# Four stages of a twelve-stage decoder kernel: pieces issued by due times, and 23 instead of 24 expert tiles

## The reference, cut to what matters

```python
x = x + _L0_attn_ref(_layernorm(x), ...)      # "memory attention", stage 0
x = x + _L0_xattn_ref(...)
x = x + _L0_ffn_ref(_layernorm(x), ...)       # 4 of 32 experts, stage 2
...
x = x + _L2_ffn_ref(_layernorm(x), ...)       # 1 of 8 experts, stage 8
...
x = x + _L3_ffn_ref(_layernorm(x), ...)       # low-rank layer, stage 11

# stage 2, routing:  scores = sigmoid(tokens @ router.T); best 2 of 4 groups by the sum of
#   their top 2; top 4 experts inside them; weights normalised, times 2.5.
#   Each expert: down(silu(gate x) * up x). A shared expert is added for every token.
# stage 8, routing:  top1 = argmax(x @ gate_W + gate_b)
#   each expert: gelu(x W1[e] + b1[e]) W2[e] + b2[e], only for its own tokens
# stage 11:
logits = einsum('bsd,ed->bse', x, gate_w) + gate_b
top_v, top_i = top_k(softmax(logits), 2);  val_sum = top_v.sum(-1)
for e in range(8):
    gate = (top_i == e).sum(-1) * val_sum
    h = relu(x @ wi.T + bi + (x @ lora_A[e].T) @ lora_B[e].T)      # rank 16, 1024 wide
    out += gate[..., None] * (h @ wo.T + bo)
```

## Time and profile before

| | |
|---|---|
| median of 3 runs | 4128.17 us (4126.56 to 4131.38) |
| profiled execution, own time | 4137.42 us |
| its span, first to last instruction | 4135.9 us |
| granted PE clock, mean | 0.873 |
| PE, DVE, ACT, POOL busy | 3217.4, 2401.6, 1643.8, 1412.9 us |

### The profile page before, as it was taken

The page is one execution under the profiler, slowest core; times in us unless marked ns, Lnnn a source line. Parts: engine busy times, 40 slices in busy tenths (PEclk is TensorE's granted clock), DMA queues, the critical chain, the costliest instruction groups (busy, mean ns, idle before and its releaser), DMA issues. The chain is left out here.

```text
span 4135.9 us, 53041 instructions
## 1 busy us (share of the span) xinstructions
PE 3217.4 (78%) x17661; PEld 2052.2 (50%) x17661; DVE 2401.6 (58%) x6477; ACT 1643.8 (40%) x3713; POOL 1412.9 (34%) x1086
## 2 busy tenths in 40 slices
PE   5888888676890678777699999478779677768898
PEld 3666666554660223322466666345656423325655
DVE  6787887247333799999343443534542258875543
ACT  3566665111120455454244444415602144436511
POOL 3666666210436254555222222301010135540110
PEclk7888888788995799999899999788969878889999
DMA  2000000300444000000000000011121200000000
GB/s 95 5 7 9 6 9 6 138 11 13 118 114 134 17 0 0 0 0 0 16 8 1 1 1 1 11 50 64 40 81 32 59 22 1 0 29 2 2 1 21
DMA packets 71175, 116.36 MB, mean 28 GB/s; under 512 B 28704, under 2 KB 58552, under 8 KB 68160
## 3 DMA queue, kind: packets, MB, share of 16 engines
q1 hardware_dynamic: 61312, 86.76, 6.2%
q0 software_dynamic: 9600, 26.23, 2.6%
HBM read 88.84 MB, written 24.12 MB: 27 GB/s over the span
## 5 line engine op out<-in xcount | busy, mean ns | idle before, releaser
L1210 POOL TENSOR_TENSOR L_attn_state<-L_attn_state,L_attn_ccol 128x1024 f32<-128x1024 f32 x192 | 458.4, 2389 | 456.1 <-DVE L_attn_state L1203 353.4
L1168 PE MATMUL bank<-L_attn_state,ident 128*128 128x512 f32 x768 | 416.2, 668 | 107.3 <-POOL L_attn_state L1210 72.4
L1203 DVE TENSOR_TENSOR_SCAN L_attn_state<-L_attn_decay,bank 128x1024 f32<-128x1024 f32 x192 | 438.6, 2284 | 22.7 <-ACT L_attn_decay L1179 3.5
L1179 ACT ACTIVATE L_attn_decay<-L_attn_dt,L_attn_A 128x512 f32<-128x512 f32 x384 | 256.2, 716 | 206.3 <-DVE L_attn_state L1203 163.3
L1168 PEld LDWEIGHTS bank<-L_attn_state,ident 128*128 128x128 f32 x768 | 152.1, 210 | 279.6 <-issue 123.6
L1107 POOL TENSOR_TENSOR L_xattn_prob<-L_xattn_prob,L_xattn_inv 128x1024 f32<-128x1024 f32 x64 | 121.1, 1893 | 411.9 <-DVE L_xattn_inv L1090 411.9
L1195 DVE TENSOR_TENSOR bank<-L_attn_dtx,bank 128x1024 f32<-128x1024 f32 x192 | 235.6, 1227 | 28.9 <-PE bank L1162 23.7
L1162 PE MATMUL bank<-L_attn_parts,L_attn_select 96*128 96x512 bf16 x384 | 145.4, 418 | 126.7 <-DVE bank L1195 110.1
L1185 ACT COPY L_attn_ccol<-bank 128x512 f32<-128x512 f32 x192 | 110.8, 577 | 208.4 <-PE bank L1162 191.5
L2813 POOL TENSOR_TENSOR L_attn_t<-L_attn_t,L_attn_base 128x1024 f32<-128x1024 f32 x96 | 183.2, 1909 | 21.6 <-DVE L_attn_base L2762 21.6
L1162 PEld LDWEIGHTS bank<-L_attn_parts,L_attn_select 96*128 96x128 bf16 x384 | 38.2, 104 | 291.1 <-DVE bank L1195 178.2
(11 more groups left out here) (599 smaller groups left out, 7551.0 us busy)
## 6 DMA issues: line engine op xcount, KB each, us to landing
L_ffn_ew<-in_L_ffn_experts SPq DMA_DIRECT2D x4, 3072.0 KB, 21.2
L_ffn_made<-L_ffn_yout SPq DMA_DIRECT2D x24, 512.0 KB, 3.0
L_ffn_w<-in_L_ffn_w SPq DMA_DIRECT2D x4, 2048.0 KB, 14.6
L_xattn_ctx<-in_ctx_rows SPq DMA_DIRECT2D x3, 2048.0 KB, 8.7
L_ffn_rows<-L_ffn_xh SPq DMA_DIRECT2D x8, 512.0 KB, 2.9
L_ffn_made<-L_ffn_yout SPq DMA_DIRECT2D x12, 256.0 KB, 2.1
L_attn_rows<-in_x SPq DMA_DIRECT2D x16, 128.0 KB, 6.8
turned<-L_attn_rows SPq DMA_DIRECT2D x16, 128.0 KB, 2.3
```

Source lines behind the costliest of these rows:

```text
L1168: t = pe.matmul(self.y[unit % len(self.y)][m][:, :], self.c.ident[:, :], self.state[N % 3][:, m, :], start=n == 0, stop=n == 15)
L1179: t = act.activation(self.decay[N % 2][:, m, :], dt[:, m, :], ACT.Exp, scale=A[:, m, n:n + 1])
L1203: dve.tensor_tensor_scan(flat(self.state[N % 3]), flat(self.decay[N % 2]), flat(self.drive), 0.0, ALU.mult, ALU.add).then_inc(*self.scanne ...
L1210: pool.tensor_tensor(state[:, :, :], state[:, :, :], self.ccol[N % 2][:, :].unsqueeze(1).broadcast_to([P, 2, GT]), ALU.mult).then_inc(*sel ...
```

## The change

The four stages get their order from tables of due times. A step name that several engines shared is split, so that each engine's part has a due time of its own (`gate`/`logits`, `turn`/`turned`, `up`/`relu`, `out`/`outed`, `top`/`raise`, `base`/`shift`, `exp`/`pick`, `rcopy`/`keep`, `choose`/`hold`, and others). In lora h1 gets a second buffer, and ACT's first relu of a group waits for `out` of two groups before. top1 works on 23 tiles, and the last tile, now without a partner, is written alone. The operations themselves are the same.

```diff
+LORA_BY_GROUP = {"root": -11.65, "stats": -11.01, "norm": -10.84, "turned": (-8.79, -7.89), "turn": (-7.92, -7.03), "logits": -7.82, "choose": -7.11,
+                 "weigh": -7.06, "shift": -6.92, "gate": -6.45, "masked": -5.12, "down": -4.01, "flipped": (-3.3, -1.98), "flip": (-2.23, -1.48),
+                 "up": (-0.86, 1.09, 2.5, 3.04, 3.91, 4.05, 7.46, 8.3), "relu": (-0.68, 1.15, 1.2, 2.49, 4.13, 7.01, 7.89, 8.47),
+                 "add": (-0.12, 0.46, 1.08, 3.47, 4.05, 5.58, 6.15, 8.66), "out": (9.27, 12.19), "outed": (11.22, 12.32)}
...
-    h1, h2 = s.sb("h1", [P, FC, GT]), [s.sb(f"h2{n}", [P, GT]) for n in range(3)]
+    h1, h2 = [s.sb(f"h1{n}", [P, FC, GT]) for n in range(2)], [s.sb(f"h2{n}", [P, GT]) for n in range(3)]
...
-        yield "stats", 0
-        yield from front(0)
-        for g in range(NGROUP):
...
+        yield "begin", 0
+        yield from as_due(due_by(LORA_BY_GROUP, 10, range(NGROUP)))
...
-            if g and m == 0:
-                act.wait_ge(*out.filled(2 * g - 1))
+            if g >= 2 and m == 0:
+                act.wait_ge(*out.filled(2 * (g - 2) + 1))
...
+BY_UNIT = {"score": -0.87, "scopy": 0.32, "top": 0.35, "raise": 0.75, "shift": 0.93, "total": 1.06, "spare": 1.15, "base": 1.24, "log": 1.4,
+           "pick": 1.73, "exp": 1.96, "turn": 2.1, "recall": 2.48, "tcopy": 2.66, "keep": 3.3, "rcopy": 3.55}
+BY_BLOCK = {"xturn": -6.43, "norm": -5.99, "xcopy": -5.4, "qsum": -3.59, "square": -3.4, "scale": -3.17, "qmul": -3.06, "out": 12.98, "y": 13.45,
+            "ynorm": 14.61, "store": 14.84}
+BY_HALF = {"query": (-5.65, -3.93), "qadd": (-4.64, -3.76), "qturn": (-2.92, -2.69), "qcopy": (-2.53, -0.82), "pair": (8.53, 9.32),
+           "sm": (9.18, 9.42), "mix": (9.59, 10.53), "oT": (10.38, 12.85), "den": (10.65, 12.66)}
...
+        due = [(n + at, key, n) for key, at in BY_UNIT.items() for n in range(UNITS)]
+        due += [(chunks * a + at, key, a) for key, at in BY_BLOCK.items() for a in range(NSEQ)]
+        due += [(chunks * a + at, key, 2 * a + half) for key, both in BY_HALF.items() for a in range(NSEQ) for half, at in enumerate(both)]
...
+        yield from (step for step in as_due(due) if step not in done)
...
+ONE_BY_GROUP = {"stats": -2.74, "norm": -2, "turn": (-1.67, -1.09), "root": -1.62, "turned": (-0.76, -0.76), "logits": -0.67, "gate": -0.38,
+                "choose": -0.28, "flip": 0.23, "flipped": 0.31, "owe": (0.82, 0.86), "owed": (0.91, 1.24), "hold": 4.02}
...
-def top1(c, s, w, name, experts=8, ff=1024, tiles=24):
+def top1(c, s, w, name, experts=8, ff=1024, tiles=23):
...
-        elif what == "down" and n % 2:
+        elif what == "down" and (n % 2 or n == tiles - 1):
+            first = n - n % 2
             sp.wait_ge(*side.emptied(side["down", n]))
-            sp.dma_start(made[n - 1:n + 1].rearrange("a t d -> t a d"), yout[n // 2 % 2][:, :, :]).then_inc(*made_out[n // 2 % 2].up(16))
+            sp.dma_start(made[first:n + 1].rearrange("a t d -> t a d"), yout[n // 2 % 2][:, 0:n - first + 1, :]).then_inc(*made_out[n // 2 % 2].up(16))
...
+FOUR_BY_GROUP = {"root": -5.55, "stats": -1.69, "norm": -1.21, "turn": (-1.07, -0.95), "turned": (-0.84, -0.61), "gate": -0.64, "sigmoid": -0.58,
+                 "silu": (-0.56, 0.05), "shared_up": (-0.29, -0.2), "choose": -0.2, "lift": (0.14, 0.17), "shared_down": (0.3, 0.59),
+                 "lower": (0.52, 1.02), "hold": 1.12}
...
+    def routing():
+        return as_due(due_by(FOUR_BY_GROUP, 1, range(NGROUP)))
```

More of the change, by code:

```diff
@@ L2446, in order @@
-        yield from behind
+        first = [(key, 0) for key in ("norm", "xturn", "xcopy", "query")] + [("keys", j) for j in range(4)]
+        yield from first + [("qadd", 0), ("query", 1), ("qadd", 1), ("square", 0), ("qsum", 0), ("scale", 0), ("qmul", 0), ("qturn", 0), ("qcopy", 0), ("qturn", 1), ("qcopy", 1),
+                            ("norm", 1), ("score", 0), ("scopy", 0), ("score", 1), ("res", 0), ("bres", 0)] + [("vals", j) for j in range(4)]
+        due = [(n + at, key, n) for key, at in BY_UNIT.items() for n in range(UNITS)]
@@ L2808, in gpsimd @@
             norm.root(n + 1)
-        elif what == "base":
+        elif what == "shift":
             pool.wait_ge(*spared.at(n))
@@ L2817, in gpsimd @@
             pool.tensor_tensor(mine, mine, flat(t[n % RING][:, 1, :, :]), ALU.subtract).then_inc(*picked.up())
-        elif what == "rcopy" and not value(n):
+        elif what == "keep" and not value(n):
             a, ch = divmod(n, chunks)
@@ L2870, in top1 @@
     wide = [P, GROUP, E]
+    def routing():
+        return as_due(due_by(ONE_BY_GROUP, 1, range(NGROUP)))
     def order():
         yield "begin", 0
-        yield "stats", 0
-        for g in range(NGROUP):
-            yield "norm", g
-            if g + 1 < NGROUP:
-                yield "stats", g + 1
-            yield "turn", 2 * g
-            yield "turn", 2 * g + 1
-            yield "gate", g
-            yield "choose", g
-            yield "flip", g
-            yield "owe", 2 * g
-            yield "owe", 2 * g + 1
+        yield from routing()
         yield from lists.order()
@@ L2908, in fills @@
             yield (what, n), {"turn": "av"[n % 2], "turn_h": "a"}.get(what, "v")
-    order_of_fills = [(what, n) for g in range(NGROUP) for what, n in
-                      (("turn", 2 * g), ("turn", 2 * g + 1), ("gate", g), ("flip", g), ("owe", 2 * g), ("owe", 2 * g + 1))]
+    order_of_fills = [step for step in routing() if step[0] in ("turn", "gate", "flip", "owe")]
     order_of_fills += [("total", 0), ("rank", 0), ("owner", 0), ("list", 0), ("match", 0), ("bias", 0)]
@@ L3004, in scalar @@
     def scalar(what, n):
-        if what == "turn" and n % 2 == 0:
+        if what == "turned" and n % 2 == 0:
             at = side["turn", n]
@@ L3035, in vector @@
             norm.apply(n, lambda b: row(GROUP * n + b), lambda b: xh[n % 2][:, b, :])
-        elif what == "turn" and n % 2:
+        elif what == "turned" and n % 2:
+            at = side["turn", n]
             if n >= 2:
@@ L3321, in scalar @@
         at = side.number.get((what, n))
-        if what == "turn" and n % 2 == 0:
+        if what == "turned" and n % 2 == 0:
             empty_turn(act, act.copy, n)
-        elif what == "gate":
+        elif what == "sigmoid":
+            at = side["gate", n]
             if n:
```

196 lines of the change are left out of this document (53 added, 143 removed).

## The result

The changed kernel takes 3974.77 us (median of 4 runs, 3974.56 to 3977.42), the kernel before 4129.77 us (4 runs, three of them those of the table further up). The ratio is 0.9627, with a 95% interval of 0.961 to 0.9643: 3.7% faster, some 154 us. The prediction said 4002 us with a range of 3950 to 4065.

The account below looks back on a forecast made before the run. Stage 0 was taken as bound by PE (waits, clock 0.86) and DVE, stages 2 and 8 by routing chains. Terms -8 - 20 - 21.5 - 6.5 - 70 = -126 us gave 4128.17 - 126 = 4002 us, range 3950 to 4065.

Parts of the forecast that it names:

- Stage 11: Stage 11: holes ahead of `out` go at three group ends and the clock stays up; -20 us, bounds -13 and -23.
- The rival in which the clock doesn't follow: Stage 11, lower bound: only the three 4.4 us holes go, -13 us; no chance given.
- Stage 2, routing: Stage 2 routing: next group's pieces fill DVE's waits, 17.5 us per group; -21.5 us, bounds -12 and -25.
- The sum of the three starts: Stage 2 routing: starts of the choice over three groups, 3 x 17.5 less the last group's missing statistics, 51.7 us.
- Stage 8, routing: Stage 8 routing: DVE stands 9 us on the first row copy, then groups overlap; -6.5 us, bounds +2 and -13.
- Stage 0: Stage 0: both PE waits lose their cause, blocks 38.0 us instead of 42.55; -70 us over 15.5 blocks, bounds -25 and -130.
- the 2.7 for the logarithm: Stage 0: DVE waits 0.9 us for the logarithm in half of the units, 2.7 us per block.
- the 1.2 for `oT`'s reciprocal: Stage 0: `oT` directly behind `top` while its reciprocal on ACT follows `rcopy`, some 1.2 us per block.
- rival C: Stage 0 reaches DVE's bound: DVE 95% full, clock 1.00, -103 instead of -70, 3969 us; chance 0.14.
- The row that spoke against: Stage 0: DVE's L2762 takes 148 to 1243 ns while POOL subtracts; slow stretches grow in shorter blocks, so 34.05 is kept.
- B: Stage 0 gains little: late `pair` holds `sm`, then `base` and the unit chain; 20 us gain, 4052 us; chance 0.22.
- D: Stage 0, slower: a chain through ACT and POOL closes over more than 7.09 us per unit; 4138 us at 7.8; chance 0.04.

Follow-up runs that it names:

- experiment 5: Changed kernel with stage 8's 8 MB of w2 loads issued behind the second copy of rows instead of ahead of the first; 3964.06 us, ratio 0.961.
- s_base: Changed kernel with `base` put behind the next `top` and `low` on DVE; mean unit 6.4 us, total time not in the text.
- s_low1: Changed kernel with `low` behind `spare`, `exp` ahead of `raise` on ACT, `pick` behind the next `shift`; PE clock 0.82, total time not in the text.
- the last one: Changed kernel with w2 loads behind the second copy of rows, and `low` split off behind the piece following `top`; 3978.68 us, ratio 0.9655.
- s_pick: Changed kernel with POOL's `pick` behind the next unit's `shift` instead of ahead of it; 53.9 us per block, total time not in the text.
- s_turn2: Changed kernel with the first `qturn` of a block moved behind `score`, ahead of `recall` and `pair`, restoring PE's wait for `qmul`; 4052.05 us, ratio 0.9822.
- experiment 3: Three variants of the changed kernel that move DVE's or POOL's small pieces in stage 0: s_base, s_pick and s_low1; none has a shorter block.
- experiments 4 and 6: 4: s_base with `scopy` ahead of `exp` on ACT, 4006.16 us. 6: changed kernel with w2 loads behind the second row copy and `low` later, 3978.68 us.

## Why the prediction was right, and where it was off

*Tiles.* Predicted -8.0, measured -8.3: one steady period of 7.98 us.

*Stage 11.* Predicted -20, measured -21.0 between the two traces and -20.9 alone (-17.8 by device time, with an interval of some 5 us to either side). The reason held: holes gone, clock 1.00, and the last group's wait kept, 2.1 us instead of 4.4. The rival in which the clock doesn't follow (-13) is out.

*Stage 2, routing.* Predicted -21.5, measured -17.6 between the two traces, -20.4 in the trace of the part alone. The sum of the three starts, 51.7, is 52.3 in most traces of this order, so it held there. In the changed kernel's own it is 54.9, with a last group of 20.0: `gate` is queued behind `shared_down`, which waits for `lift`, and both run at the lower clock. The sum had neither that wait nor the clock.

*Stage 8, routing.* Predicted -6.5 with a stand of 9 us, measured -10.9 with one of 9.67 (-9.1 by device time of the part alone). The mechanism was right, and experiment 5 priced it. What differs is the walk around it: the copy is issued 5.5 us ahead of the first `gate` (3.0 before), so the second `gate` came 17.3 us behind the first (19.8 by hand), and the groups behind it are 9.1 to 9.7 us apart.

*Stage 0.* This is the step that was mis-sized: -70 predicted, -97.5 alone. The mechanism was right as to PE: both its waits went, the clock rose from 0.86 to 1.00, and PE's 32.0 us came out as 32.8. DVE did not come out above PE: both are busy 65.5 to 65.7 of 72.6 us, and which of them, or which circle of waits, sets the 36.3 us is not shown. The sum 34.05 + 2.7 + 1.2 = 38.0 us per block came out as 36.3 = 32.8 of work + 2.6 of waits in the list above (per block 1.3 for `out`, 0.7 for `query`, 0.6 for ACT) + 0.8 of small gaps, counted on DVE. Term by term: DVE's work was 1.2 too high; the 2.7 for the logarithm were 0, since `spare`, 2.1 us, stands ahead of `base` in every unit; the 1.2 for `oT`'s reciprocal were 0; and the waits for PE were not in the sum, though the kernel before has one of them too (15.0 us in 14, for `out`). 1.7 us in 15.8 blocks are 27 us, as much as the forecast's whole error of 27; the errors of the other parts (4 us too little in stage 8, 1 in stage 11, up to 4 too much in stage 2) nearly cancel, which is luck. So rival C, with -103 for this stage, had the better size. What held the forecast back was the logarithm's wait of the earlier trace rows, carried over from an order that has no `spare` between `total` and `base`.

*The row that spoke against.* "34.05 is kept for DVE, the slow instructions stay as slow" was nearly right as a sum: `low` and `base` together took 1.57 us per unit before (791 + 780 ns on the mean) and 1.42 after (1082 + 337). It was wrong to see it as a matter of POOL's share of the time. What counts is which POOL instruction is running when the DVE piece starts. Whether the time so lost is worth anything stays open: three kernels that took some or all of it away (s_base, s_low1 and the last one) had longer blocks, but each by an order that brought waits of its own.

*Rivals.* B did not occur in the change; s_pick and s_turn2 show that its circle is real, at 53.9 and 41.2 us per block. D did not occur: the unit takes 6.04 us. Its kind of circle, through POOL, ACT and DVE, is seen in s_base.

## What to carry to other kernels

Before shortening the fullest engine, find the circle of waits that a unit goes round, through each engine's queue: moving one small step by 0.12 of a unit cost some 40 us, another by 0.22 some 280, although the first took 3.5 us per block of work off a 90% full engine. Price a wait of PE as three things, the wait, the slow stretch behind it, and whoever waits for the late piece; here the slow stretch was 3.2 of the 5.0 us by which the block grew. And when a step moves ahead in an order, look at what it waits for in the DMA queues as well: issuing two small copies ahead of 8 MB of loads shortened that routing by 6 to 10 us, and cost nothing in the tiles behind it.

## What the hardware did that was not expected

`low` and `base`, DVE instructions with two inputs in SBUF, stand to the very end of the POOL instruction that is running: `low` takes 226 ns alone and 1000 when it meets `shift`, whose end it shares to 0.1 us. Instructions with one input, `MAX8`, or with one of two in a bank, `sm`, don't: in the timelines of experiment 3 eight `MAX8` take 1.12 us beside `pick`, and in the changed kernel 1.10 beside `shift`; two `sm` take 1.29 us in s_base while `shift` runs, and 1.27 elsewhere. The Trainium skill (SBUF — State Buffer, SBUF: two separate sides) states that the pair of ports is an exclusive lock, which whichever of the two starts first holds for its whole instruction; for a DVE instruction with two SBUF inputs it says so against a POOL instruction that reads SBUF. The traces agree where POOL is first. For the other order there is one case: a `shift` of the kernel before, at 102.95 us, took 2.62 us instead of 1.90 while `qmul`, begun at 102.17, ran to 103.81. The page says more than the one that the prediction used.

PE idles of 0.6 to 1.2 us, several per block, left the granted clock at 1.00 in stage 0 of the changed kernel, and at 0.98 in the kernels of experiments 4 and 6; with one of 4.3 us per block it was 0.87 to 0.93 over stretches of 100 us.
